# A state-space mixer whose decay differences come from DMA-loaded rows and are made before the projection tiles

## The reference, cut to what matters

```
g = 8 groups, 16 heads each, 128 tokens per chunk, 8 chunks
gate, hBC, dt = split(LN(x) @ in_proj)            # per group: 1024 gate, 1024 hidden, 128 B, 128 C columns
hs, B, C = silu(conv4(hBC))
A_cum = cumsum(dt * A) in a chunk                 # one row of 128 per head and chunk
L[l, s] = exp(A_cum[l] - A_cum[s]) if s <= l else 0
Y = (C B^T * L) (hs * dt)  +  (C state) * exp(A_cum)  +  hs * D
y = rmsnorm_per_group(Y * silu(gate)) * norm_w
x += y @ out_proj
```

## Time and profile before

| | |
|---|---|
| median of 3 runs | 3361.16 us |
| the profiled execution itself, its span | 3364.29 us, 3362.5 us |
| PE, DVE, ACT, POOL busy | 88%, 67%, 31%, 20% of the span |
| granted TensorE clock over the span | 0.95 |
| the 64 steps of the mixer | from 144.99 us (first L503) to 2467.8 us |
| one group of eight steps | 293.6 us |

### The profile page before, as it was taken

One profiled execution on the slowest core, in us unless ns is written; L12 is line 12 of the kernel. 1 busy time (PEld: TensorE's weight loads), 2 busy tenths in 40 slices (PEclk: granted clock), 3 DMA queues, 4 the chain that ended last, 5 costly groups with the idle time before them and its releaser, 6 DMA issues. The chain is left out here.

```text
span 3362.5 us, 39926 instructions
## 1 busy us (share of the span) xinstructions
PE 2949.6 (88%) x11856; PEld 1634.5 (49%) x11856; DVE 2268.2 (67%) x3758; ACT 1034.2 (31%) x2401; POOL 661.0 (20%) x440
## 2 busy tenths in 40 slices
PE   2799898989989898998989899899869997888889
PEld 1344444544444454444445445444448553333478
DVE  4676767777677777767777776767545555777464
ACT  1232222223222222322322332232222234656421
POOL 1122122222212222221222222122222100000021
PEclk7899999999999999999999999999879898999989
DMA  5010020010002001000200100010010231111000
GB/s 168 13 29 8 1 70 17 4 58 26 8 1 71 17 4 59 25 7 1 71 16 4 61 25 5 1 54 1 1 66 0 104 112 38 33 33 37 10 7 19
DMA packets 48134, 107.78 MB, mean 32 GB/s; under 512 B 9104, under 2 KB 18400, under 8 KB 45248
## 3 DMA queue, kind: packets, MB, share of 16 engines
q1 hardware_dynamic: 42624, 102.47, 9.2%
q10 hardware_dynamic: 5312, 2.92, 0.3%
HBM read 86.23 MB, written 19.14 MB: 31 GB/s over the span
## 5 line engine op out<-in xcount | busy, mean ns | idle before, releaser
L439 PE MATMUL bank<-xnT,wh 128*128 128x512 f32 x1280 | 592.7, 607 | 124.3 <-DVE sg L842 92.2
L528 PE MATMUL bank<-wg,xnT 128*128 128x512 f32 x1024 | 482.8, 616 | 0.0
L580 PE MATMUL bank<-wo,ggT 128*128 128x512 f32 x1024 | 466.1, 609 | 0.5 <-ACT ggT L689 0.5
L439 PEld LDWEIGHTS bank<-xnT,wh 128*128 128x128 f32 x1280 | 241.3, 194 | 411.1 <-issue 278.4
L733 DVE SCALAR_TENSOR_TENSOR cacc<-raw,cwh,cacc 128x512 f32<-128x512 f32 x480 | 390.3, 813 | 17.0
L580 PEld LDWEIGHTS bank<-wo,ggT 128*128 128x128 f32 x1024 | 201.9, 198 | 237.8 <-issue 232.4
L528 PEld LDWEIGHTS bank<-wg,xnT 128*128 128x128 f32 x1024 | 193.5, 199 | 197.7 <-issue 197.7
L503 PEld LDWEIGHTS bank<-xch,em 128*128 128x128 f32 x2048 | 237.4, 194 | 55.1 <-issue 52.3
L503 PE MATMUL bank<-xch,em 128*128 128x64 f32 x2048 | 243.4, 278 | 6.4 <-DVE em L791 2.4
L928 POOL TENSOR_TENSOR yt<-yt,hd 128x1024 f32<-128x1024 f32 x64 | 153.4, 2396 | 474.3 <-DVE yt L814 399.8
L638 ACT COPY xs<-bank 128x512 f32<-128x512 f32 x128 | 74.6, 583 | 546.6 <-PE bank L469 546.6
...
## 6 DMA issues: line engine op xcount, KB each, us to landing
...
```

Source lines behind the costliest of these rows:

```text
L439: mm = nc.tensor.matmul(BA[bank][:, :], wh[:, j, k, :], xnT[:, k, h * HALF:(h + 1) * HALF], start=(k == 0), stop=(k == KC - 1))
L528: mm = nc.tensor.matmul(BA[b][:, :], xnT[:, k, ttok], wg[:, k, u * 512:(u + 1) * 512], start=(k == 0), stop=(k == KC - 1))
L580: mm = nc.tensor.matmul(BA[b][:, :], ggT[:, j, :], wo[:, j, :], start=(j == 0), stop=(j == JT - 1))
```

## The change

The bf16 parts of A_cum are now transposed once, in setup (eight float32 matmuls at new line L277 of the kernel after, then `part`, a table of head by token, with its negative), and written to DRAM as `rows_scratch`. Before each chunk SP loads the 2 x 3 rows of its 16 heads into `RW`, six partitions beside which rows of ones stand; the other partitions are zero. There is one `RW`; its next load is issued when all four differences of the chunk before are done. For each quarter `pe_diff` now does one bf16 matmul of 512 columns that puts -1e30 where s > l (identity times `negq`), and adds, for each of its 4 heads, one bf16 matmul of 128 columns with weights of its own. The exp reads the PSUM bank directly; the minimum, the masking product, the selector product and the small copies on DVE are gone; one copy of 256 columns (C B^T and B together) stays. In `pe_slot` the first two quarters stand ahead of tile 0 and the last two between tile 1 and the transposes of the gated result. The waits of `pe_pre` and `pe_hidden` for the convolved tiles are cut to those that each one reads.

```diff
         def pe_pre(pe, g, z):
...
-            dv_act.wait(pe, (2 * g + h) * PT + PT)
-            pe.wait_ge(d_pk[h], 32 * g + 32)
+            dv_act.wait(pe, (2 * g + h) * PT + 2)
...
-            nc.tensor.transpose(sm[0:PK, 2 * P:2 * P + P // 2].bitcast(BF16),
-                                pk[:, h, c, O_PARTS:PACK].bitcast(BF16), identb[:, :]).then_inc(pe_sm.sem, 1)
         def pe_hidden(pe, g, z, u):
...
+            dv_act.wait(pe, (2 * g + h) * PT + 2 + 4 * (u + 1))
...
         def pe_diff(pe, g, z, quarters):
             n = 8 * g + z
-            dv_sm.wait(pe, 5 * n + 5)
+            if quarters[0] == 0:
+                pe.wait_ge(d_rw, 32 * n + 32)
...
             for q in quarters:
-                dv_mn.wait(pe, 4 * n + q - 1)
-                nc.tensor.matmul(BD[q % 2][:, :], Lp[:, :], Rp[:, q * 512:(q + 1) * 512],
-                                 start=True, stop=True).then_inc(pe_df.sem, 1)
+                ac_ex.wait(pe, 4 * n + q - 1)
+                nc.tensor.matmul(BD[q % 2][:, :], identb[:, :], negq[:, :], start=True, stop=False)
+                for i in range(QH):
+                    hh = slice((q * QH + i) * P, (q * QH + i + 1) * P)
+                    mm = nc.tensor.matmul(BD[q % 2][:, i * P:(i + 1) * P], RW[:, 0, hh], RW[:, 1, hh],
+                                          start=False, stop=(i == QH - 1))
+                mm.then_inc(pe_df.sem, 1)
...
-            tile(0)
             if not last:
                 pe_diff(pe, *nxt, (0, 1))
+            tile(0)
             tile(1)
+            if not last:
+                pe_diff(pe, *nxt, (2, 3))
             dv_gg.wait(pe, n + 1)
...
             tile(2)
-            if not last:
-                pe_diff(pe, *nxt, (2, 3))
             tile(3)
...
         def ac_exps(act, g, z, quarters):
             n = 8 * g + z
+            pe_yd.wait(act, 2 * n)
             for q in quarters:
-                dv_mn.wait(act, 4 * n + q + 1)
-                nc.scalar.activation(em[:, q, :], em[:, q, :], ACT.Exp).then_inc(ac_ex.sem, 1)
+                pe_df.wait(act, 4 * n + q + 1)
+                nc.scalar.activation(em[:, q, :], BD[q % 2][:, :], ACT.Exp).then_inc(ac_ex.sem, 1)
...
         def dv_small(dve, g, z):
...
-            nc.vector.tensor_copy(pS[:, :], sm[0:PR, 2 * P:2 * P + P // 2].bitcast(BF16)).then_inc(dv_sm.sem, 1)
-            nc.vector.tensor_copy(Lp[64:PK, :], sm[64:PK, 2 * P:2 * P + P // 2].bitcast(BF16)).then_inc(dv_sm.sem, 1)
-            nc.vector.tensor_copy(Bs[:, z % 2, :], sm[:, P:2 * P]).then_inc(dv_sm.sem, 1)
             dv_M.wait(dve, 4 * n)
-            nc.vector.tensor_tensor(CBm[:, :], sm[:, 0:P], mask[:, :], ALU.mult).then_inc(dv_sm.sem, 1)
-            dv_sm.wait(dve, 5 * n + 1)
-            nc.vector.tensor_tensor(Rp[0:PR, :].rearrange("p (h l) -> p h l", h=HG),
-                                    selb[:, :].rearrange("p (h l) -> p h l", h=HG),
-                                    pS[:, :].unsqueeze(1).broadcast_to([PR, HG, P]), ALU.mult).then_inc(dv_sm.sem, 1)
+            nc.vector.tensor_copy(BC[:, z % 2, :], sm[:, 0:2 * P]).then_inc(dv_sm.sem, 1)
...
-                nc.vector.tensor_scalar(em[:, q, :], BD[q % 2][:, :], 0.0, None, ALU.min).then_inc(dv_mn.sem, 1)
...
+                def load_rows(g, z):
+                    for side, at in ((1, 0), (0, 1)):
+                        sp.dma_start(RW[PARTS * side:PARTS * side + PARTS, at, :].rearrange("i (h l) -> i h l", h=HG),
+                                     rows_dram[side, :, bass.ds(g * HG, HG), z * P:(z + 1) * P]).then_inc(d_rw, 16)
...
+                def next_rows(g, z):
+                    pe_df.wait(sp, 4 * (8 * g + z + 1))
```

More of the change, by code:

```diff
@@ L178, in mixer @@
             pack = sb(c0, "pack", [P, NT, G, PACK])
+            part = sb(c0, "part", [P, 2, PARTS, T], BF16)
             XCUT = ((0, 2), (2, NT // 2), (NT // 2, NT))
@@ L198, in _ @@
                     load_out(sp, 0)
-                    sp.wait_ge(v_ch, 26)
+                    sp.wait_ge(v_ch, 22)
+                    sp.dma_start(rows_dram.rearrange("s i h t -> h (s i) t"), part[:, :, :, :].rearrange("h s i t -> h (s i) t")).then_inc(s_pack, 16)
+                    sp.wait_ge(v_ch, 25)
                     for g in range(G // 2):
                         sp.dma_start(pack_dram[g], pack[:, :, g, :]).then_inc(s_pack, 16)
-                    sp.wait_ge(s_pack, 16 * G)
+                    sp.wait_ge(s_pack, 16 * (G + 1))
                 @block.scalar
@@ L271, in _ @@
                         mm = nc.tensor.matmul(BANK[4 + i][:, :], mask[:, :], rem[:, i * 512:(i + 1) * 512],
+                                              start=True, stop=True)
+                    for z in range(NT):
+                        mm = nc.tensor.matmul(BANK[z // CH][:, (z % CH) * P:(z % CH + 1) * P], rem[:, z * P:(z + 1) * P], mask[:, :],
                                               start=True, stop=True)
@@ L343, in _ @@
                     chain(o)
-                    dve.wait_ge(p_cst, 2)
+                    for i in range(2):
+                        o = nc.vector.tensor_copy(v2[:, i * 512:(i + 1) * 512], BANK[i][:, :])
+                    chain(o)
+                    src = v2
+                    for i in range(PARTS):
+                        chain(nc.vector.tensor_copy(part[:, 0, i, :], src[:, :]))
+                        if i < PARTS - 1:
+                            chain(nc.vector.tensor_tensor(rem[:, :], src[:, :], part[:, 0, i, :], ALU.subtract))
+                            src = rem
+                    chain(nc.vector.tensor_scalar(part[:, 1, :, :], part[:, 0, :, :], -1.0, None, ALU.mult))
+                    dve.wait_ge(p_cst, 1)
                     z4 = lambda ap: ap.rearrange("p (z g h) -> p z g h", z=NT, g=G)
-                    pb = pack[:, :, :, O_PARTS:PACK].bitcast(BF16)
                     chain(nc.vector.tensor_copy(pack[:, :, :, O_DT:O_DT + HG], z4(dt[:, :])))
@@ L447, in pe_pre @@
             b = (5 * z) % 2
-            dv_act.wait(pe, (2 * g + h) * PT + PT)
-            pe.wait_ge(d_pk[h], 32 * g + 32)
+            dv_act.wait(pe, (2 * g + h) * PT + 2)
             ac_yT.wait(pe, 2 * (n - 1))
             ac_xs.wait(pe, 2 * n)
-            dv_sm.wait(pe, 5 * n)
-            if z == 0 and isinstance(g, int) and g == 0:
-                pe.wait_ge(s_cst, 32)
+            dv_sm.wait(pe, n)
             tok = slice(c * P, (c + 1) * P)
@@ L465, in pe_hidden @@
             h, c = z // CH, z % CH
+            dv_act.wait(pe, (2 * g + h) * PT + 2 + 4 * (u + 1))
             if u == 1:
-                dv_sm.wait(pe, 5 * n + 4)
+                dv_sm.wait(pe, n + 1)
             for i in range(4):
@@ L519, in state @@
                     dv_yd.wait(pe, 2 * n + u + 1)
-                    nc.tensor.matmul(BY[u][:, :], Bs[:, z % 2, :], xd[:, u * 512:(u + 1) * 512],
+                    nc.tensor.matmul(BY[u][:, :], BC[:, z % 2, P:], xd[:, u * 512:(u + 1) * 512],
                                      start=True, stop=True).then_inc(pe_st.sem, 1)
@@ L671, in tanh @@
                     ac_tile_tanh(act, step, mine[r])
+            if not last:
+                ac_exps(act, *nxt, (0, 1))
             copy(0)
@@ L677, in ac_slot @@
             if mine:
-                if not last:
-                    ac_exps(act, *nxt, (0, 1))
                 copy(1)
@@ L691, in ac_slot @@
                 o.then_inc(ac_yT.sem, 1)
-            if not mine and not last:
-                ac_exps(act, *nxt, (0, 1))
             copy(2)
@@ L775, in dv_xdt @@
                 .then_inc(dv_xc.sem, 1)
-        def dv_min(dve, g, z, quarters):
-            n = 8 * g + z
-            pe_yd.wait(dve, 2 * n)
-            for q in quarters:
-                pe_df.wait(dve, 4 * n + q + 1)
-                nc.vector.tensor_scalar(em[:, q, :], BD[q % 2][:, :], 0.0, None, ALU.min).then_inc(dv_mn.sem, 1)
         def dv_masked(dve, g, z):
             n = 8 * g + z
-            dv_sm.wait(dve, 5 * n + 4)
+            dv_sm.wait(dve, n + 1)
             for q in range(NQ):
@@ L863, in silu @@
                     dv_silu_tile(dve, step, mine[r])
-            if not last:
-                dv_min(dve, *nxt, (0, 1))
             conv(0)
@@ L869, in dv_slot @@
             silu(0)
-            if not last:
-                dv_min(dve, *nxt, (2, 3))
             conv(2)
@@ L990, in _ @@
                     load_pack(g + 1, 1)
+                for z in range(NT - 1):
+                    next_rows(G - 1, z)
             @block.gpsimd
@@ L1043, in prologue @@
                     dv_xdt(dve, 0, 0)
[L1044 removed]
                     dv_masked(dve, 0, 0)
[L1046 removed]
+                run(dve, dv_slot, prologue, (dv_cv, dv_act, dv_sm, dv_xc, dv_M, dv_yo, dv_yd, dv_sg, dv_gg, dv_st, dv_out, dv_r))
     if debug is not None:
```

77 lines of the change are left out of this document (38 added, 39 removed).

## The result

| | before | after | forecast |
|---|---|---|---|
| median, us | 3361.44 (3358.73 to 3364.86) | 3236.89 (3233.11 to 3237.73) | 3237 (3185 to 3288) |
| ratio after / before | | 0.9627 (0.9610 to 0.9643) | |
| profiled execution: time, span, us | 3364.29, 3362.5 | 3237.73, 3235.9 | |
| mean granted clock | 0.950 | 0.966 | |
| end of the mixer's first step to the end of its last, us | 2281.8 | 2157.7 | |

What lies ahead of the end of the mixer's first step gave 2.5 us; what follows the mixer takes 894.6 us in both.

A forecast was written before the change was run, and what follows sets the result against it. PE was taken as the bound, losing time to waits and slow clock. Seven groups at -15.3 us (-107), the last -13.5 and setup -3 gave -124: 3240 us profiled, median 3237, range 3185 to 3288.

The forecast's parts named there:

- PE's added work: Each step's four quarters on PE: 1.78 us against 0.87, less one transpose, so +0.85 us a step at 2.4 GHz.
- Rival 3: Weight loads of the heads' matmuls aren't hidden: 1.58 us more a step, 3322 us; chance 0.04.
- Steps 1, 2, 5, 6: Steps of a group with a 3.08 us wait ahead of tile 0: left-over convolution ends sooner, net -1.7 us a step.
- Clock of z = 1: Step z = 1 of a group: its slow clock stretch goes with the 3.08 us waits, -1.6 us.
- Step 3: Step z = 3 of a group: no wait for the left-over silu, one slow stretch left, -3.1 us.
- Step 7: Step z = 7 of a group: PE waits about 0.4 us instead of 3.96, one slow stretch left, -5.5 us.
- rival 1: The clock comes back whole and L849 runs clear of POOL's work: -174 us, 3187 us; chance 0.14.
- Last group: The eighth group, whose steps 4 to 6 have no tiles and give -2.1 us each: -13.5 us in all.
- Setup and prologue: Ahead of the steps: added matmuls +4, packed table -2, `pe_pre` wait about 5 less; together -3 us, between +4 and -6.
- Loads: A step's two loads of rows, issued a step ahead, late only at z = 0: cost 0, at most 3 us times 7.
- Rival 4: Slower: the load of rows is exposed and PE stands 3 us in every step, 3429 us; chance 0.04.
- Rivals 2 and 5: 2: clock stays as it is, 3278 us, chance 0.12. 5: another chain sets tile 0, 3319 us, chance 0.06.

The follow-up runs named there:

- exps first: Changed kernel with ACT's first two exps ahead of its second `xs` copy in steps without tiles: 3204.71 us, ratio to before 0.9539.

## Why the prediction was right, point by point

- *PE's added work* (+0.85 a step): +0.81 and +0.89 in steps 0 and 4, and the heads' matmuls with weights of their own stand 0.056 us apart. Rival 3 (exposed weight loads) fell. (The forecast's way to 0.056 was loose: 0.65 less 0.16 over eight is 0.061. In the earlier trace rows the starts are 0.091 apart once and 0.056 from then on.) On this the rule of the Trainium skill, "TensorE: Matmul & The Clock Gate", section "The mechanism", that a load overlaps with running matmuls only when the row group differs, isn't borne out here: all rows are used, a load is 98 ns long, and the matmuls stand 56 ns apart. The same section also lets a load into the background weight buffer be pulled ahead, and that leaves room for it; no run here tells whether it is the way.
- *Steps 1, 2, 5, 6* (-1.7): the chain was the right one and so was the cause of its end, POOL's addition, which the run without that addition showed. The size was off, and this is the step that failed here: "ends 2.12 us behind the addition" was taken from a step where the convolution's first operation starts 0.17 us ahead of POOL and gets through. Here POOL is ahead by 0.17, the first operation is caught, and the end is 2.65 us behind: 1.01 us of wait and not 0.5, 30 steps, 14 us too much gain.
- *Clock of z = 1* (-1.6): its step fell by 1.70 more than its neighbours. Right.
- *Step 3* (-3.1): -3.4. The form was as forecast (a wait of 0 to 1.5 ahead of the transposes: 1.53; then one for ggT: 1.14; some slow stretches left). With waits alike in each group it lasts 28.6, 30.2 or 31.7, by whether a slow stretch follows and how long.
- *Step 7* (-5.5): -8.3, the case I had priced as "L849 clear of POOL" with the clock whole (-8.0) and put into rival 1. Two steps failed. L563 was to follow 4.43 us behind the gate's half "as before", and with it L849 at its held-up length (2.79); it follows 2.97 behind, since DVE now starts first (1.23). Which engine starts first is decided by 0.2 us, and the sum had no term for that. And one slow stretch (1.7 us) was counted as left, where the slow time in step 7 is 0 in all seven groups. The run without POOL's addition prices the first alone: with POOL first and no slow stretch step 7 lasts 27.09, 1.65 more. Together 20 us over seven groups, which hid the 14 above.
- *Last group* (-13.5): -8.2. Steps 4 to 6 were to give 2.1 each and gave 2.1, 0.65 and 0.4: waits of 1.5 and 1.2 us stay in each, and two of these steps still run at 0.94. Step 3 gave 1.8 and not 3.1, with 6.8 us of slow time left.
- *Setup and prologue* (-3): -2.5 up to the end of the first step. Its terms (+4, -2, -5) were not measured apart.
- *Loads* (0): no step shows PE waiting for a row. Rival 4 fell. Rivals 2 and 5 fell with the clock and with tile 0 (rivals 3 and 5 were priced with 32 steps of the kind 1, 2, 5, 6; there are 30). Rival 1 came true in step 7 and not in step 3.

The mechanisms of the waits are shown by runs that take away or put back one cause. That the parts don't add because of the clock is shown as far as its record goes: with half of the slow time off, they add to within 4 us. What decides whether a given wait has a slow stretch behind it is open: step 3 has waits of 0.41, 1.53 and 1.14 us in each of the first seven groups, and slow time of 0, 3.4 or 6.8 us. Open too is whether the new arithmetic is worth having once all orders are in, since the kernel before wasn't run with the exps first.
